# The first stage's output projection and norm moved inside the causal attention block, and a window stage that starts on a quarter of its tokens

## Time and profile before

| | us |
|---|---|
| median of 3 runs (lowest, highest) | 2311.33 (2304.25, 2318.38) |
| the profiled execution's own time | 2307.12 |
| its span, first to last instruction | 2305.3 |
| first work of the next block's TensorE after the attention block's last divide | 401.68 |
| last normalize ends, window stage's first turn begins | 418.39, 419.18 |
| first projection of the window stage begins | 427.37 |

### The profile page before, as it was taken

One profiled execution on the slowest core, in us unless ns is written; L12 is line 12 of the kernel. 1 busy time (PEld: TensorE's weight loads), 2 busy tenths in 40 slices (PEclk: granted clock), 3 DMA queues, 4 the chain that ended last, 5 costly groups with the idle time before them and its releaser, 6 DMA issues. The chain is left out here.

```text
span 2305.3 us, 55541 instructions
## 1 busy us (share of the span) xinstructions
PE 2014.6 (87%) x20349; PEld 1353.3 (59%) x20349; DVE 1809.4 (78%) x3609; ACT 1665.7 (72%) x3163; POOL 1267.5 (55%) x1132
## 2 busy tenths in 40 slices
PE   5788888579999999999999999999999999984283
PEld 3233332346766776776767677677767776673152
DVE  4666660699999999999999999999999999834623
ACT  2265555378888888888898888888888888864123
POOL 4400000477777677767777776776677677711052
PEclk8799997699999999999999999999999999996587
DMA  6321100211111121111211111101211111100511
GB/s 160 97 58 26 23 2 2 66 36 38 29 38 29 30 86 29 38 29 38 77 38 29 39 57 49 38 29 38 77 38 29 33 35 32 35 20 26 186 35 66
DMA packets 70562, 107.36 MB, mean 47 GB/s; under 512 B 20887, under 2 KB 47774, under 8 KB 68734
## 3 DMA queue, kind: packets, MB, share of 16 engines
q1 hardware_dynamic: 68262, 100.87, 15.2%
q0 software_dynamic: 1280, 2.62, 0.4%
q10 hardware_dynamic: 752, 0.33, 0.1%
HBM read 41.60 MB, written 12.26 MB: 23 GB/s over the span
## 5 line engine op out<-in xcount | busy, mean ns | idle before, releaser
L1446 POOL TENSOR_TENSOR qk<-rot_cos,rot_sin 128x512 f32<-128x512 f32 x256 | 323.2, 1274 | 160.3 <-DVE rot_sin L1247 160.3
L1245 DVE TENSOR_TENSOR rot_cos<-pA,layer_tab 128x512 f32<-128x512 f32 x384 | 262.8, 684 | 65.6 <-ACT sq L1086 58.7
L1456 POOL TENSOR_TENSOR qk<-qk,rnorm 128x512 f32<-128x512 f32 x256 | 262.9, 1043 | 88.0 <-DVE rnorm L1280 88.0
L382 ACT ACTIVATE probs_by_key<-pT 128x512 f32<-128x512 f32 (+3 forms) x384 | 176.9, 489 | 155.2 <-PE pT L298 119.8
L1086 ACT ACTIVATE sq<-pA 128x512 f32<-128x512 f32 x384 | 228.4, 595 | 55.9 <-PE pA L873 46.1
L439 DVE TENSOR_REDUCE minus_max<-pS 128x1 f32<-128x1024 f32 (+7 forms) x256 | 184.3, 753 | 106.4 <-PE pS L270 105.8
L1257 DVE TENSOR_REDUCE sumsq<-sq 128x8 f32<-128x512 f32 x384 | 253.4, 670 | 14.8 <-ACT sq L1086 14.6
L1247 DVE TENSOR_TENSOR rot_sin<-pA,layer_tab 128x512 f32<-128x512 f32 x384 | 260.8, 679 | 0.0
L1146 ACT ACTIVATE probsT<-pD 64x512 f32<-64x512 f32 x384 | 226.4, 589 | 43.8 <-PE pD L914 40.3
L1463 POOL TENSOR_TENSOR probs<-probs,row_inverse 128x1024 f32<-128x1024 f32 x96 | 182.7, 1904 | 104.9 <-DVE row_inverse L1316 104.9
L1106 ACT ACTIVATE qT<-pC 64x512 f32<-64x512 f32 x384 | 225.9, 588 | 7.3 <-PE pC L888 0.5
(11 more groups left out here) (313 smaller groups left out, 4619.4 us busy)
## 6 DMA issues: line engine op xcount, KB each, us to landing
v_shifted<-v SPq DMA_DIRECT2D x96, 384.0 KB, 3.5
v_shifted<-v SPq DMA_DIRECT2D x95, 128.0 KB, 3.4
q_stack<-stacked SPq DMA_DIRECT2D x24, 192.0 KB
k_stack<-stacked SPq DMA_DIRECT2D x24, 192.0 KB
W_ahead<-in_Wqkv_dram SPq DMA_DIRECT2D x12, 384.0 KB
layer_weights<-in_Wqkv_dram SPq DMA_DIRECT2D x12, 384.0 KB
stacked<-part SPq DMA_DIRECT2D x32, 128.0 KB, 2.4
tokens_in<-tokens SPq DMA_DIRECT2D x2, 1024.0 KB
```

Source lines behind the costliest of these rows:

```text
L1245: dve.tensor_tensor(t1[c % 2][:, :].rearrange("p (h g d) -> p h g d", g=2, d=32), a, tabl[s % 2][:, j].unsqueeze(1).broadcast_to([P, 8, 2, ...
L1446: pool.tensor_tensor(qk(s, c), t1[c % 2][:, :], t2[c % 2][:, :], ALU.add).then_inc(added[c], 1)
L1456: pool.tensor_tensor(v, v, rn[p % 2][:, o:o + 8].unsqueeze(2).broadcast_to([P, 8, DH]), ALU.mult).then_inc(scaled[c], 1)
```

## The change

Nothing of the arithmetic changes but where and by which engine some of it is done.

- `project_out_normalized` is gone. Its work stands in `causal_from_tokens`, in tiles that exist already: turned `w_out` in `wT`, turned `O` in `xT`, the sums in `raw[0]`, the squares in `raw[1]`, and the projections in four banks of `S`.
- Its first half (`n` 0 and 1, the first sequence) is put between the chunks of iteration 8: TensorE turns `w_out` at `u` 2, turns at 5 and 11, projects at 8 and 14 (`PROJECT_AT`). VectorE makes the copies there (before: ScalarE), adds the residual, and after `divide(6)` centres, squares (three instructions of 128x512 for a chunk; before: ScalarE), makes the variance and normalizes.
- Its second half (`n` 2 and 3) follows the last divide, without an end of a block between. ScalarE copies and squares as before. The order on VectorE is now: both residuals and means, then variance 2, normalize 2, variance 3, normalize 3.
- `turn_output(7)` waits for `added` 2, since its tile shares banks with the first projections.
- In `window_layers` the turned tokens go to banks that round 0 and 1 do not use. TensorE begins round 0 when the first four tiles are copied (`xT_ready` 1) and two clears are done (`zeroed` 2), and waits for the rest ahead of rounds 1 and 2. ScalarE copies the first four tiles without waiting for GpSimd, does its round 0, and copies the other twelve tiles ahead of its round 1. VectorE does its small clears first; it still waits for all seven before its own round 0. SyncE waits for `zeroed` 7 in place of 1.

```diff
+        PROJECT_AT = {2: ("wo", 0), 5: ("turn", 0), 8: ("project", 0), 11: ("turn", 1), 14: ("project", 1)}
@@ tensor
+                    if it == GROUPS and u in PROJECT_AT:
+                        first_half(*PROJECT_AT[u])
                     if 2 <= it and u == OUT_AT:
                         turn_output(it - 2)
+            pe.wait_ge(s_free, output_at(GROUPS - 1) + 1)
+            pe.wait_ge(exp_done, GROUPS * NT)
+            for n in (2, 3):
+                turn_out(n, ST[n - 2])
+            for n in (2, 3):
+                project_out(n)
@@ scalar
             keep_output(GROUPS - 1, 1)
+            for n in (2, 3):
+                act.wait_ge(o_turned, n + 1)
+                act.activation(oT[:, four(n), :], ST[n - 2][:, :].rearrange("p (t n) -> p t n", t=CT), AF.Copy).then_inc(ot_kept, 1)
+            for n in (2, 3):
+                act.wait_ge(centred, n + 1)
+                for t in range(CT * n, CT * n + CT):
+                    act.activation(squares[:, t, :], Z[:, t, :], AF.Square, bias=negm[:, t:t + 1], accum_out=sq[:, t:t + 1])\
+                        .then_inc(squared, 1)
@@ vector
             for it in range(GROUPS + 2):
                 if it == GROUPS:
                     keep_maxima(GROUPS - 1)
+                    first_half()
...
+                    if it == GROUPS and u == OUT_AT:
+                        for n in range(2):
+                            centre(n)
+                            square(n)
+                            variance(n)
+                        for n in range(2):
+                            normalize(n)
...
+            for n in (2, 3):
+                residual(n)
+                centre(n)
+            for n in (2, 3):
+                variance(n)
+                normalize(n)
@@ window_layers, tensor
-            for n, bank in enumerate((A[0], A[1], C[0], C[1])):
+            for n, bank in enumerate((Db[0], Db[1], F[0], F[1])):
...
-            pe.wait_ge(xT_ready, 4)
-            pe.wait_ge(const_loaded, 32)
-            pe.wait_ge(zeroed, 7)
             for r in range(PAIRS + 5):
+                if r == 0:
+                    pe.wait_ge(xT_ready, 1)
+                    pe.wait_ge(zeroed, 2)
+                if r == 1:
+                    pe.wait_ge(const_loaded, 32)
+                    pe.wait_ge(zeroed, 7)
+                if r == 2:
+                    pe.wait_ge(xT_ready, 4)
                 pe_body(pe, r)
@@ window_layers, scalar
+            keep_tokens(0, Db[0])
             for r in range(PAIRS + 5):
+                if r == 1:
+                    for n, bank in ((1, Db[1]), (2, F[0]), (3, F[1])):
+                        keep_tokens(n, bank)
+                    act.wait_ge(zeroed_p, 3)
+                    act.wait_ge(zeroed, 7)
                 act_body(act, r)
```

More of the change, by code:

```diff
@@ L83, in causal_from_tokens @@
         OS = sb("out_rows", [P, SEQ])
+        negm, sq, ve, rstd, half = (sb(n, [P, TILES]) for n in (
+            "negative_mean_a", "square_sum_a", "var_eps_a", "rstd_a", "root_power_a"))
+        woT, oT = wT[:, 0, :], xT[:, :].rearrange("p (t n) -> p t n", t=TILES)
+        Z, squares = (r[:, :, :].rearrange("p m (t n) -> p (m t) n", n=D) for r in raw)
         den = sb("denominator", [P, 2, TB * GH])
@@ L214, in _ @@
                     load_stacks(g - 1 + SLOTS_G)
+            for n in range(4):
+                sp.wait_ge(normed, CT * (n + 1))
+                sp.dma_start(w["aside"][:, four(n), :], X[:, four(n), :]).then_inc(env["aside_stored"], 16)
         @block.tensor
@@ L313, in values, with turn_out, project_out, first_half @@
                 mm.then_inc(pv_done, 1)
+            def turn_out(n, out):
+                for j in range(CT):
+                    mm = pe.transpose(out[:, j * P:(j + 1) * P], O[:, CT * n + j, :], ident[:, :])
+                mm.then_inc(o_turned, 1)
+            def project_out(n):
+                pe.wait_ge(ot_kept, n + 1)
+                for j in range(CT):
+                    mm = pe.matmul(Y_BANKS[n][:, j * P:(j + 1) * P], oT[:, CT * n + j, :], woT, start=True, stop=True, skip_group_check=True)
+                mm.then_inc(y_ready, 1)
+            def first_half(kind, n):
+                if kind == "wo":
+                    pe.wait_ge(env["out_loaded"], 16)
+                    pe.transpose(SPARE[:, 0:P], env["wo"][:, :], ident[:, :]).then_inc(wo_turned, 1)
+                elif kind == "turn":
+                    pe.wait_ge(wo_kept, 1)
+                    ge(pe, added, n)
+                    turn_out(n, SPARE)
+                else:
+                    project_out(n)
             done = 0
@@ L543, in _ @@
                 copy_values(g)
[L546 to L625, removed]
@@ L626, in _ @@
             pool.memset(half[:, :], -0.5).then_inc(half_set, 1)
             pool.wait_ge(half_set, 1)
-            for n in range(CH):
+            for n in range(4):
                 pool.wait_ge(eps_done, n + 1)
[L630 to L645, removed]
-            def normalize(n):
-                dve.wait_ge(rooted, n + 1)
-                for t in range(CT * n, CT * n + CT):
-                    dve.tensor_scalar(X[:, t, :], Z[:, t, :], negm[:, t:t + 1], rstd[:, t:t + 1], ALU.add, ALU.mult).then_inc(normed, 1)
-            residual(0)
-            residual(1)
-            variance(0)
-            residual(2)
-            variance(1)
-            normalize(0)
-            residual(3)
-            variance(2)
-            normalize(1)
-            variance(3)
-            normalize(2)
-            normalize(3)
@@ L665, in causal_masks @@
+                pool.tensor_tensor(rstd[:, four(n)], ve[:, four(n)], half[:, four(n)], ALU.pow).then_inc(rooted, 1)
 def causal_masks():
@@ L847, in _ @@
             load_layer(sp, w, W[1], 1, w_loaded[1])
[L848 removed]
+            sp.wait_ge(zeroed, 7)
             for s in range(STEPS):
@@ L1218, in _, with keep_tokens @@
         def _(act):
-            act.wait_ge(zeroed_p, 3)
-            for n, bank in enumerate((A[0], A[1], C[0], C[1])):
+            def keep_tokens(n, bank):
                 act.wait_ge(x_turned, n + 1)
```

56 lines of the change are left out of this document (49 added, 7 removed).

## The result

The changed kernel takes 2292.26 us (median of 8 runs, 2286.44 to 2298.16), the kernel before 2313.43 in the 8 runs beside it. One of those took 3412.98 us and is left out of the ratio; the median of the other seven is 2311.33. The ratio is 0.9918, 95% interval 0.9896 to 0.9940: 19 us less, between 14 and 24. I had forecast 2305, 6.4 us less, in a range of 2295 to 2314; the direction was right, the size less than half. The profiled execution has a span of 2291.0 us against 2305.3.

A forecast was written before the change was run, and what follows sets the result against it. A chain, not an engine, was taken to bound tail and head, and TensorE the second pass at half clock. Tail -4.6, head -4.5 and moved work +2.7 gave -6.4 us, forecast 2305, range 2295 to 2314.

The forecast's parts named there:

- Part 1, the tail: From last divide to last normalize: the tail ends 4.6 us earlier, bounds 3.5 to 6.
- Variance 3 stood behind normalize 2: In VectorE's stream in the tail: the third chunk's squares, ready at 410.5, wait 0.9 us.
- Part 2, the head: Window stage's start: first projection 3.7 us after the first turn instead of 8.19, 4.5 us gained, bounds 2.8 to 5.5.
- the table: GpSimd's table, ready at 419.5, was to leave the first rotation 1.7 us; releasing that rotation would prove the forecast wrong.
- Part 3, the price of the moved work: First half's projection work moved into iteration 8: costs 2.7 us, ends 0 and 6.25.
- I take 2.7, between 2.2 and 3.2: Iteration 8: 2.2 us of shown TensorE work, plus 1.0 if chunks are pushed behind the clock's fall.
- is as thin as it was: Iteration 8 behind `u` 14: the added work makes it denser only up to there, 20 us behind unchanged.
- the sum: Whole kernel: -4.6 - 4.5 + 2.7 = -6.4 us; 2300.7 on the profiled time, 2304.9 on the median.
- price of 2.2: Iteration 8 at full clock: 3.5 us of moved TensorE work shows at 64%, costing 2.2 us.
- The clock holds: Rival: denser iteration 8 carries full clock through the second pass; -19 us, 2292 on the median; chance 0.14.
- The clock falls early: Rival: clock falls before the moved work, at chunks 320 to 326; +5.9 us, 2313.0 on the profiled time; chance 0.24.
- The head's gain: Rival: another wait takes the window stage's gain, leaving -1.9 us, 2309.4 on the median; chance 0.14.

The follow-up runs named there:

- e12: Light filler: changed kernel plus 192 unused columns ahead of the first 9 and last 43 thin chunks, variance 3 ahead of normalize 2; 2300.89 us, 0.9948 of before.
- e4: Changed kernel plus one unused bf16 product of 256 columns ahead of each of the 66 thin chunks; 2292.64 us, 0.9930 of before.
- e1: Kernel before with only the window stage's new head; 2313.87 us, 0.9999 of before.
- e9: Change's attention block with the window stage's old head; 2305.07 us, 0.9958 of before.
- e11: Kernel before, unchanged, profiled again and not timed; turned maxima of the last group to last divide 51.7 us, 17.1 of it at half clock.
- e16: Kernel before, unchanged, third profile and not timed; turned maxima of the last group to last divide 49.1 us, 6.8 of it at half clock.
- e5: Kernel before with the last group's second pass repeated six times (288 chunks) behind the last turned output, no filler; 1.0917 of before.
- e8: Kernel before with the last group's second pass repeated six times, plus one unused bf16 product of 256 columns ahead of each repeated chunk; 1.0828 of before.
- e10: Changed kernel, unchanged, profiled and timed again; 2291.77 us, 0.9911 of before.
- e14: Changed kernel with variance 3 ahead of normalize 2 and 26 unused bf16 products of 512 columns behind the last projection; 2286.93 us, 0.9908 of before.
- e6: Kernel before with the last group's second pass repeated six times, plus 6 unused f32 transposes before every fourth or fifth chunk; 1.0891 of before.
- e2: Kernel before plus unused TensorE work of the moved kinds at the moved steps of iteration 8; 2314.18 us, 0.9999 of before.
- e13: Same program as e12, run again on another chip; 2299.20 us, 0.9923 of before.
- e3: Changed kernel with the moved TensorE work cut to about a quarter, its result wrong; 2301.51 us, 0.9944 of before.
- e7: Kernel before with the last group's second pass repeated six times, plus 3 unused f32 products of 128x128 before every fourth or fifth chunk; 1.0915 of before.

## Why the prediction was wrong

**Part 1, the tail: right.** -4.6 forecast, -5.4 measured. The block's end cost 0.80 as before. The projections ran faster than I took them (16 instructions in 3.03 us, for my 4.1), since the clock came up within them. Variance 3 stood behind normalize 2 as said; the order of e12 takes it out, and its tail is 9.9 for the 10.6 of e4, both with the projections at full clock.

**Part 2, the head: right.** -4.5 forecast; -4.75 to the first projection and another 0.4 to the first rotation. That rotation was released by ScalarE's squares, not by the table, which was ready at 413.7, 1 us ahead. e1 and e9 show the part by itself and its absence.

**Part 3, the price of the moved work: wrong, and the cause of the miss.** The step that failed is "I take 2.7, between 2.2 and 3.2", with the clause that the rest of iteration 8 "is as thin as it was" and so falls as before. That is the mis-sized term: the sum left the clock as it was, and the clock is what the work changes. Seven profiles have the plain stretch (before, e11, e16, and e5 to e8, which are the kernel before up to there): B is 49.1 to 55.9, mean 54.1. The four with the change's attention block up to there (changed, e10, e9, e14) have 50.2, 48.8, 48.8 and 48.3, mean 49.0. That is -5.1 where I had +2.7, 8 us of error in a forecast that was 12.7 off by the median.

Means over so few profiles could be chance, since e16 lies among the changed ones. Profiles whose clock fell at the same places ahead of A (within 1 us) are the better comparison, because there B repeats:

| falls ahead of A begin at | plain | with added work |
|---|---|---|
| 25, 36, 63, 233 us | before 55.8, e8 55.9 | e14 48.3, e4 50.1 |
| 27, 65, 160, 314 us | e5 55.4, e6 55.5 | e2 47.5, e12 48.8, e13 48.8 |

In both rows the added work takes 6 to 8 us off. e3, whose last falls ahead of A begin at 161 and 315, lies between with its 53.3. The changed kernel's first profile has no such partner. Nearest is e16, which in B has the same two falls of 3.4 us. There the plain stretch is the shorter one, 49.1 for 50.2: where the clock falls no more than that, the work costs about 1 us, by one profile of each. So the price of 2.2 was too high as well, and the gain hangs on a clock that would else stay low for long. The first pair of profiles set a long fall against an execution that might have had short ones anyway; by itself it would prove nothing. The window over B of e14, beside that of before in the earlier trace rows:

```profile
344.80:393.10 48.30, 39.22 (x290) 15.59 (x290) 13.27 (x32) 31.69 (x70) 2.07 (x2) 0.97 0.04 13
```

What differs is where and for how long the clock falls. In the plain profiles and e1, counted from A, a fall begins at 4 us in four and at 25 in three, and lasts 10 to 68 us; one (e16) has two of 3.4 us. In the nine profiles with moved work or filler at full rate none begins before 19.8, and none lasts longer than 7 us. The quartered work (e3) lies between: one fall of 3.4 us at 4, one of 17 at 31. How the work does this is open. Of the added work of e2 and e3 only a single turn comes in the first 4 us after A: TensorE was busy for 3.28 of these 4.1 us in e2, where the clock then did not fall, and for 3.28 in e3 and 3.07 in e5, where it did. So it is not shown that the work prevents the early fall's start; that it ends it sooner, e3 against e5 suggests. Nor do the runs settle why the later falls became short, when the work is already over: the long repeats show only that the stretch falls and recovers by itself if left thin, and never falls if filled.

**The rivals.** "The clock holds" gave 2292 on the median, and 2292.26 was measured; I had given it 0.14. It was right in kind, not in the detail: the clock doesn't hold, it falls briefly. My case against it was that the 20 us behind `u` 14 are unchanged. I used one execution's fall at 370.3 as the kernel's behaviour, though I had noted a spread of 14 us between three runs. That its total agrees to 0.3 us is luck in part: it had 4 us for a full clock in the tail and at its edges, of which 0.8 came. "The clock falls early" does happen: it is what e1, e5, e6 and e7 do, in the kernel before; of the profiles with A at 357 and the added work at full rate (e2, e12, e13) none has it. The head's gain was not taken.

**The sum.** By means over the profiles: B -5.1, tail -5.0, head -4.7, round 0 -0.8 (20.7 to 21.1 before, 20.1 after, from first projection to the first Newton step), together -15.6; the measured 19 has an interval of 14 to 24. The profiles of the two kernels alone (three and two) are 13.0 us apart from A to the end, 1957.8 for 1944.8. By their totals the two parts alone, 0.9999 (e1) and 0.9958 (e9), each within 0.0035, make up 10 us and not 19; the noise is wide enough for that to be chance.

**What stays open.** Over the eighteen profiles A is 345 to 349 us in nine, 357 to 358 in seven, and 364 to 365 in two; what differs is the clock. Up to A the clock is 0.95 where A is late (the windows of e2 and e11 above), for 0.99 where it is early, as in the kernel before:

```profile
107.00:345.30 238.30, 213.46 (x1646) 88.19 (x1645) 154.11 (x252) 142.20 (x311) 4.32 (x6) 0.99 0.11 27
```

The code there is the same in all kernels. This is worth 12 us, more than the tail and the head together. How often it is late may be bound to the program: of the changed kernel's 20 runs one is above 2298.5 us, of the light filler's 22 runs 13 are (7 of 12, then 6 of 10), though by its profiles it is 4 us shorter from A on. On the chip that ran e10 and e12 it is 1 of 12 against 7 of 12. But the 2298.5 was chosen after the runs, and A itself is known for one execution of each kernel only, so this is not shown. What would decide it, I don't know; nothing ahead of A was changed. The part of the measured 19 us that the sum lacks may be this, or noise.

## What to carry to other kernels

Where TensorE's granted clock is not a flat 1.00 in a stretch, don't price added or removed TensorE work at one clock level. Look at where the clock falls, in more than one execution, and make "the work changes the clock" the first case of the sum. Work that is moved into a stretch in which TensorE waits for another engine may cost less than nothing, if the clock falls there without it, and work taken out of such a stretch may cost more than it saves. When totals are noisy by more than the effect, cut profiles at fixed instructions, compare stretch by stretch, and compare executions whose clock went the same way up to that stretch.

## What the runs showed of the hardware

- A steady stream in which TensorE is busy for 10.87 of 13.70 us at full clock falls to 1.2 GHz and returns, on and off, in falls of 10 to 55 us (e5). No idle gap between its TensorE instructions is longer than 0.79 us.
- f32 transposes, f32 products and thin bf16 products, all unused, kept the clock at full for some 200 us (e6 to e8).
- Executions of the same code whose clock had fallen at the same places up to A repeated the time of the next stretch, B, within 0.1 us (before and e8, e5 and e6, e9 and e10, e12 and e13), though in e5 and e6 the falls within B lie at different places.
- 26 bf16 products of 512 columns took 5.78 us in the idle time at the end of a block. The next block's 16 transposes then ran at 2.4 GHz, 1.9 us in place of 3.7, though 1.55 us of idle time and a block's end lay between (e14).
